# A new order of work around each exchange, with a quarter of it issued by ScalarE, in a fused attention and linear kernel

## What is computed

```python
xn = layernorm(x)
q = (xn @ wq.T)                        # 16 heads, 128 "nope" + 64 rotary columns
kv_lat, k_pe = split(xn @ wkv_a.T)     # 128 + 64
q_lat = einsum('bshd,hdc->bshc', q_nope, wkv_b_h[:, :128])
kv_cache = rmsnorm(kv_lat, kv_norm_w)
scores = (q_lat . kv_cache + rope(q_pe) . rope(k_pe)) * SCALE, causal
attn = softmax(scores)
out_lat = einsum('bsht,btc->bshc', attn, kv_cache)
out = einsum('bshc,hdc->bshd', out_lat, wkv_b_h[:, 128:]) @ wo.T
result = x + out + (xn @ ternary(weight).T + bias)
```

## Time and profile before

| | |
|---|---|
| runs of the kernel | 2119.6, 2119.89, 2128.14 us; median 2119.89 |
| the profiled execution | 2115.17 us, span 2113.1 us |
| PE busy | 1803.1 us (85%) |
| PEld, DVE, ACT, POOL busy | 1523.3, 1208.9, 853.5, 1004.4 us |
| mean granted clock of TensorE | 0.92 |
| DMA queue of SP | 48.6% of 16 DMA engines' span |
| DMA queue of ACT | 5.5% |

### The profile page before, as it was taken

The page is one execution under the profiler, slowest core; times in us unless marked ns, Lnnn a source line. Parts: engine busy times, 40 slices in busy tenths (PEclk is TensorE's granted clock), DMA queues, the critical chain, the costliest instruction groups (busy, mean ns, idle before and its releaser), DMA issues.

```text
span 2113.1 us, 28101 instructions
## 1 busy us (share of the span) xinstructions
PE 1803.1 (85%) x9326; PEld 1523.3 (72%) x9326; DVE 1208.9 (57%) x2801; ACT 853.5 (40%) x1358; POOL 1004.4 (48%) x635
## 2 busy tenths in 40 slices
PE   6997888778989979889888898788898888888885
PEld 5786666657777767777777777677677777777775
DVE  5764566646666655656465555455555555555552
ACT  4552443433444433344444434243443434334342
POOL 4763444434554554454444545344444544445443
PEclk9888899989999999999999999898999989999998
DMA  6992555547656565654444535546455455453544
GB/s 226 356 315 100 147 141 157 162 133 186 169 151 161 148 190 138 168 134 116 119 125 121 136 102 132 158 98 174 112 121 125 104 128 123 114 131 95 127 105 102
DMA packets 127183, 309.11 MB, mean 146 GB/s; under 512 B 29442, under 2 KB 41987, under 8 KB 125508
## 3 DMA queue, kind: packets, MB, share of 16 engines
q1 hardware_dynamic: 117152, 273.20, 48.6%
q10 hardware_dynamic: 9892, 34.18, 5.5%
HBM read 113.28 MB, written 34.60 MB: 70 GB/s over the span
## 4 chain that ended last, share of the span: by engine, by line
PE 28%; issue 20%; POOL 13%; SPq 12%; ACT 8%; DMA 5%; DVE 5%; POOLq 0%; ACTq 0%; DVEq 0%
SPq L986 11%; PE p_score L1101 10%; PE p_out L1121 9%; POOL pT L1367 7%; DMA pT<-turned 5%; PE p_result L1133 4%; DVE turned L1192 3%; ACT pT_h L1286 3%; PE p_lat L1081 3%; ACT probs L1275 3%; POOL qp_l L1356 3%; POOL qp_l L1359 3%; PE p_rot L1081 2%; ACT qp_h L1310 2%; DVE probs L1170 1%
## 5 line engine op out<-in xcount | busy, mean ns | idle before, releaser
L1367 POOL TENSOR_TENSOR pT<-pT,pT_h 128x1024 fp32r<-128x1024 f32 x320 | 684.1, 2164 | 576.4 <-ACT pT_h L1286 574.3
L1170 DVE TENSOR_SCALAR_CACHE_REDUCE probs<-p_score 128x512 f32<-128x512 f32 (+3 forms) x640 | 382.8, 602 | 617.7 <-PE p_score L1101 435.3
L1121 PE MATMUL p_out<-pT_h,V_h 128*128 128x256 f32 (+3 forms) x1024 | 327.9, 320 | 198.0 <-DVE o_l L1219 103.4
L1286 ACT ACTIVATE pT_h<-pT 128x1024 fp32r<-128x1024 f32 x320 | 291.4, 963 | 451.7 <-DMA pT<-turned 296.1
L1275 ACT ACTIVATE probs<-probs,neg_max 128x128 f32<-128x128 f32 (+15 forms) x256 | 307.0, 1199 | 378.9 <-DVE neg_max L1176 376.8
L1121 PEld LDWEIGHTS p_out<-pT_h,V_h 128*128 128x128 f32 x1024 | 213.2, 208 | 235.3 <-DVE o_l L1219 116.1
L1192 DVE STREAM_TRANSPOSE turned<-probs 128x1024 f32<-128x1024 f32 (+7 forms) x384 | 341.5, 915 | 28.2 <-ACT probs L1275 23.4
L1121 PE MATMUL p_out<-pT,V_h 128*128 128x256 f32 (+3 forms) x1024 | 323.0, 315 | 0.0
L1121 PE MATMUL p_out<-pT_h,V_l 128*128 128x256 f32 (+3 forms) x1024 | 321.8, 314 | 0.0
L1101 PE MATMUL p_score<-Kn_h,q_h 128*128 128x512 f32 (+3 forms) x640 | 249.4, 390 | 18.0 <-DVE q_l L1215 18.0
L1101 PE MATMUL p_score<-Kp,qp_h 128*128 128x512 f32 (+3 forms) x640 | 242.6, 379 | 21.3 <-POOL qp_l L1359 20.5
(11 more groups left out here) (135 smaller groups left out, 2390.0 us busy)
## 6 DMA issues: line engine op xcount, KB each, us to landing
pT<-turned SPq DMA_DIRECT2D x512, 128.0 KB, 2.3
Wq<-wq_scr ACTq DMA_DIRECT2D x63, 512.0 KB, 4.5
Wv<-wv_scr SPq DMA_DIRECT2D x63, 512.0 KB, 3.6
pT<-turned SPq DMA_DIRECT2D x256, 112.0 KB, 2.3
pT<-turned SPq DMA_DIRECT2D x256, 96.0 KB, 2.2
pT<-turned SPq DMA_DIRECT2D x256, 80.0 KB, 2.1
pT<-turned SPq DMA_DIRECT2D x256, 64.0 KB, 2.5
Wp<-wp_scr SPq DMA_DIRECT2D x31, 512.0 KB, 4.3
```

The source lines that it names most:

```text
L1121: mm = pe.matmul(out[:, :, cols, :], v[:, t, :], pt[:, :, t - first, rest, :], start=(t == 0 and a == 0), stop=(t == piece_tiles(s) - 1 an ...
L1170: dve.tensor_scalar(probs[row % ROW_RING][:, b * CW:b * CW + width], p_score[n % SCORE_RING][:, 0:width], SCALE, LOWEST, ALU.mult, ALU.max ...
L1286: act.activation(high.rearrange("p r t i q -> p r t (i q)"), low.bitcast(F32).rearrange("p r t i q -> p r t (i q)"), ACT.Copy).then_inc(p_ ...
L1367: pool.tensor_tensor(low.rearrange("p r t i q -> p r t (i q)"), low.bitcast(F32).rearrange("p r t i q -> p r t (i q)"), high.bitcast(F32). ...
```

## The change

- In the matmul queue the value groups of a piece move from units 2, 3, 4 to 3, 4, 5 in stage 3 and from units 1, 3, 5, 7 to 3, 4, 5, 6 in stage 4; stages 1 and 2 stay. The output projections of stage 4 move from units 2, 3, 4, 5 to 0, 1, 2, 2. `p_lat` moves one unit ahead in stage 4, `p_rot` ahead of the first scores in stage 1 and to unit 1 in stage 4.
- `high_group` and `low_group` move from unit 0 of slot s+2 to its unit 1 in stages 1 and 3, and from the last unit of slot s+1 to unit 0 of slot s+2 in stage 4. `split_output` and `high_output` follow the last value group: unit 0 of slot s+3 instead of unit 5 of s+2 in stage 3, unit 7 of s+2 instead of unit 0 of s+3 in stage 4.
- DVE turns the last row of a piece at unit 0 of the next slot in all stages; before at unit 1 from slot 17 on.
- ACT makes each exponential ahead of the query and rotary splits of the same unit, and that of a slot's last row at the slot's end.
- SP issues three quarters of each exchange, 12 DMAs. ACT issues the fourth with four DMAs (`exchange_last`), behind the same two waits, at unit 1 of the next slot (unit 0 up to slot 16).
- In stage 1 all five rotary operations stand in unit 0 on DVE, the sum in unit 1 and the splits in unit 2.

```diff
 def value_unit(s, k):
-    return (2 + k, 1 + k, 2 + k, 1 + 2 * k)[phase(s)]
+    return (2 + k, 1 + k, 6 - groups_of(s - 2) + k, 3 + k)[phase(s)]
...
     if k < HIGH_RING:
-        return (s + 2, 0) if phase(s + 1) in (0, 2) else (s + 1, units_of(s + 1) - 1)
+        return (s + 1, units_of(s + 1) - 1) if phase(s + 1) == 1 else (s + 2, 0 if phase(s + 1) == 3 else 1)
...
-    return 2 + i if s % 2 == 0 else i
+    return 0 if s % 2 else (2 + i if phase(s) == 2 else (0, 1, 2, 2)[i])
...
                 if 1 <= s <= SLOTS:
-                    exchange(s - 1, (2, 3))
+                    exchange(s - 1, (2,))
...
                 for u in range(units_of(s)):
+                    rotary = u == rotary_unit(s) and opens_head(s) and g % 2 and g + 1 < HEADS
+                    if rotary and s < H:
+                        project_rotary(g + 1)
                     if s < SLOTS:
                         scores(g, unit_of_head(s, u))
-                    if u == 0 and opens_head(s) and g % 2 and g + 1 < HEADS:
+                    if rotary and s >= H:
                         project_rotary(g + 1)
...
-                    if 1 <= s <= SLOTS and u == (1 if s > H else 0):
+                    if 1 <= s <= SLOTS and u == 0:
                         turn_row(head_of(s - 1), first_row(s - 1) + rows_of(s - 1) - 1)
...
+            def exchange_last(s):
+
+                g, tiles = head_of(s), piece_tiles(s)
+                act.wait_ge(blocked, QB * g + first_row(s) + rows_of(s))
+                need(act, pv_done, groups_before(s - 1) if s >= 1 else 0)
+                for r in range(4):
+                    act.dma_start(slots(pT[s % 2][96:P, :], s)[:, r, 0:tiles, :, :].bitcast(F32),
+                                  slots(turned[s % 2][32 * r:32 * (r + 1), :], s)[:, 3, 0:tiles, :, :]
+                                  ).then_inc(exchanged[s % 2], 16)
...
                 for u in range(units_of(s)):
-                    if u == query_unit(s) and g + 1 < HEADS:
-                        high_query(g + 1)
-                        if g + 2 < HEADS:
-                            load_q(g + 2)
                     for old in (s - 3, s - 2):
                         if 0 <= old < SLOTS and (s, u) == split_place(old):
                             high_output(old)
...
                             if (s, u) == high_place(old, k):
                                 high_group(old, k)
+                    if s < SLOTS and (u + 1) % (chunk_of(g) + 1) == 0 and u + 1 < units_of(s):
+                        exp_row(g, first_row(s) + u // (chunk_of(g) + 1))
+                    if u == query_unit(s) and g + 1 < HEADS:
+                        high_query(g + 1)
+                        if g + 2 < HEADS:
+                            load_q(g + 2)
                     if u == rotary_high_unit(s) and g + 1 < HEADS:
                         high_rotary(g + 1)
-                    if s < SLOTS and (u + 1) % (chunk_of(g) + 1) == 0:
-                        exp_row(g, first_row(s) + u // (chunk_of(g) + 1))
+                    if 1 <= s <= SLOTS and u == (1 if s > H else 0):
+                        exchange_last(s - 1)
+                if s < SLOTS:
+                    exp_row(g, first_row(s) + rows_of(s) - 1)
```

More of the change, by code:

```diff
@@ L179, in latent_unit, with rotary_unit @@
         return (1 + it // 2, 2 + it)[phase(s)]
-    return (it if phase(s) == 2 else 1 + it) if s < SLOTS and closes_head(s) else None
+    return it if s < SLOTS and closes_head(s) else None
 def query_unit(s):
     if s < 2 * H:
-        return (3, 6)[phase(s)]
-    return (4 if phase(s) == 2 else 5) if s < SLOTS and closes_head(s) else None
+        return (2, 6)[phase(s)]
+    return 4 if s < SLOTS and closes_head(s) else None
 def rotate_ops(s, u):
     if phase(s) == 0:
-        return ((), (0, 1, 2), (3, 4), ())[u]
-    return ((0,), (1, 2), (3, 4))[u - 1] if 1 <= u <= 3 else ()
+        return range(5) if u == 0 else ()
+    first = rotary_unit(s) + 1
+    return ((0,), (1, 2), (3, 4))[u - first] if first <= u <= first + 2 else ()
+def rotary_unit(s):
+    return 1 if phase(s) == 3 else 0
 def rotary_add_unit(s):
-    return (2 if phase(s) == 0 else 4) if opens_head(s) else None
+    return (1, 4, 4, 5)[phase(s)] if opens_head(s) else None
 def rotary_high_unit(s):
-    return (3 if phase(s) == 0 else 5) if opens_head(s) else None
+    return (2, 5, 5, 6)[phase(s)] if opens_head(s) else None
 def row_unit(s, i):
```

## The result

| | before | now | forecast |
|---|---|---|---|
| median of the runs | 2119.97 us (2119.6 to 2128.14) | 1893.19 us (1886.6 to 1894.48) | 1925 |
| ratio, 95% interval | | 0.8916 (0.8886 to 0.8946) | 0.908 |
| profiled execution, span | 2115.17, 2113.1 | 1894.48, 1892.0 | 1920 |
| PE busy | 1803.1 us (85%) | 1717.4 us (91%) | |
| mean granted clock | 0.92 | 0.97 | |

The account below looks back on a forecast made before the run. Stage 4 was held to be set by a closed loop through the exchange, not PE's work; terms -96-74-30+8-3 = -195 took the profiled 2115.17 to 1920, plus 4.7 for the median: 1925 us, 8-in-10 range 1880 to 2025.

Parts of the forecast that it names:

- The loop in stage 4: Fourth query chunk: exchange, pT_h, exp, o_h, o_l, turn, next exchange; one round of 22.3 us sets the slot.
- A: Rival, exchanges: transfers, not issues, set them, so data still lands late; 1963 us, chance 0.2.
- B: Rival, stages 3 and 4: ACT-POOL chain 1.2 us later than walked, PE waits in all 64 slots; 2022 us, chance 0.18.
- C: Rival, ACT's queue: wait for data delays exchange_last behind it, a self-feeding loop; about 2235 us, chance 0.05.
- D: Rival, stages 1, 3, 4: acc and o_l in time, no new waits; 1848 us, half of it 1887, chance 0.07.
- Stage 4: Fourth query chunk: 600 us against 695.9, from 569 of full-clock slots, 19 waiting for acc, 12 for lower clock.
- Stage 3: Third query chunk: 484 us against 557.9, from 449 of full-clock slots, 15 for o_l, 10 clock, 10 boundary.
- Stage 2: Second query chunk: 336 us against 366.5; order unchanged but for turn and exchange, pT waits mostly go.
- Stage 1: First query chunk: +8 us; per pair of slots +2.5 for acc, +0.5 for clock, -1.8 for q_l, 7 pairs.
- The quarter on ACT: Exchange issues: with all 16 on SP data lands 2.5 us later, costing 22 us in stage 3, 16 in stage 4.
- the cover: Stage 4: the exchange lands at least 1.7 us before the next slot's first pT_h wants it.
- the tail: End of the kernel, behind the stages: 3 us less for the shorter last exchange.

Follow-up runs that it names:

- Run 5: Changed kernel with the exp of a slot's last row put back behind the next slot's three pT_h, stage 4 only: 1974.61 us, ratio 0.9303.
- Run 7: Changed kernel with ACT's query and rotary splits ahead of the exp of their unit again, stage 2 only: 1882.68 us, ratio 0.8864.
- the control: The changed kernel timed again, unaltered, on the chip of the experiments: 1894.49 us, ratio 0.8936 to the kernel before.
- run 1: Changed kernel's new order with all 16 DMAs of an exchange issued on SP, none on ACT: 1906.45 us, ratio 0.897 to the kernel before.
- run 2: Kernel before, in its old order, with only a quarter of each exchange moved to ACT: 2040.87 us, ratio 0.9615.
- run 3: Kernel before with only the exp of a slot's last row moved ahead of the three pT_h, stage 4 only: 2103.58 us, ratio 0.9908.
- run 4: Changed kernel with half of each exchange, eight DMAs, issued on ACT instead of a quarter: 1944.3 us, ratio 0.9153 to the kernel before.

## Why the prediction was right, and where its terms were off

- *The loop in stage 4: right.* It said that one round of exchange, pT_h, exp, o_l and turn sets the slot and that the moves cut it. Run 5 puts one link back and loses 79 us; the windows show PE as the bound. Rivals A and B would leave a wait of ACT for data or of PE for POOL's pT in most slots; stage 4 has neither, but for one of 1.68 us at its end. C needed issues over 1.5 us; ACT's have a median of 0.635. D, with no new waits, had 1887 for half of its terms: the waits for acc and o_l did come, smaller, and their share for a lower clock did not. One reading of the prediction is wrong: the slot at clock 0.87 has one standstill, of 5.76 us, and not two. That the total is only 32 us off is in part luck: stages 1, 3 and 4 were forecast 46 us too long and stage 2 21 us too short.
- *Stage 4: 22 us too long.* PE's full-clock slots are 18.98, 17.70, 16.84 and 17.70, that is 71.2, where 71.1 was said. The wait for acc is there, but 0.94 and 0.30 us in a slot instead of 2.4, so 10 to 12 us in place of 19: 7 less. The 12 us for a lower clock behind it did not come: the slot with the wait has clock 1.00. The last 3 are slots at the stage's ends.
- *Stage 3: 14 us too long.* The wait for o_l is 1.2 us and not 1.85 (6 less), it drew no lower clock (10 less), the slots with no wait are 15.00 and 13.90 instead of 15.29 and 14.06 (6 less), and the stage's ends cost 18 and not 10 (8 more). Its row, from 870 to 1230:

```profile
PE p_result L1138 <- DVE o_l L1227: 8.2, 7, 1.2
```

- *Stage 2: 21 us too short, the worst term.* That the order is unchanged but for the turn and the exchange was wrong. The wait for pT in even slots did go, as said; but ACT's exp had moved ahead of q_h inside a unit, and PE waits for acc there in both slots, 0.86 and 0.73 us (13 us in the 8 pairs). Before, PE had one such wait in the stage, of 0.51 us. Run 7 takes this away; the kernel is 10.5 us faster for it. The rest: one slot (the fourth) where ACT waits 8.4 us for its data while the chunk's store and load run, some 5 us, and busy slots 0.4 us a pair longer, 3 us. Of this part the control has less (its stage is 353 us), so it is an estimate.
- *Stage 1: 10 us too long.* The wait of 3 us for acc was predicted at 3.2 and measured at 3.03:

```profile
363.90 0.73 PE L1138 MATMUL p_result<-Wv,o_h 128*128 128x512 f32 x2 [3.03 <-DVE acc L1241]
```

  What was left out is what it replaces. Per pair of slots the kernel before had four waits of PE, 0.88 twice for q_l, 1.62 for qp_l and 0.67 for acc; the prediction counted only the first two as going. Now there are 3.03 and 1.06: 4.1 against 4.05, and nothing is left of the 8 us. The charge for the clock was right in kind: beside four of the stage's seven standstills of 3.03 us, and beside all seven in the control, stands a stretch at 1.2 GHz.
- *The quarter on ACT: some 10 us, not 38.* The stages differ here. In stage 4 the exchange got shorter by 1.1 us (median from first issue to last landing 13.1 in run 1, 12.0 now) and not by 2.5; both queues issue more slowly side by side. And the cover was larger than walked: the slot is 17.7 us or more and not 16.4, since it has its own wait or its longer neighbour; in run 1 ACT waits for no data from 1340 to 1820. In stage 3 the exchange did get shorter by 2.2 us (12.5 and 10.3), and in run 1 ACT is late in 17 of 32 slots; but POOL's low parts still come before PE wants them, so the step that failed is the one from ACT's lateness to PE's. (The 16 us for stage 4 are also mis-added: 0.8 x 0.7 x 32 is 18.) The Trainium skill ("DMA: Bandwidth & Descriptors", Issuing engines are not separate DMA queues) lets a second issuing engine save only the sequencer's time; by it the prediction said that the 2.5 us shrink to almost nothing in stage 4. The trace agrees with the rule: what is saved is 2.2 us in stage 3 and 1.1 in stage 4, never more than the 2.5 of issuing, and stage 4 is 4 us shorter for it. What the saved time is worth depends on the order around it: in run 2, where a loop holds the exchange, about 1 us less in every slot is worth 82 us.
- *The rest:* the tail is 5.5 us shorter, where 3 was said. The stages and the tail make 27 of the 32 us; of the others most is that the median, taken 4.7 us above the profiled execution, is 1.3 below it now.

## What to carry to other kernels

When an engine's queue waits for data at a fixed place, ask which instructions behind that place make the next data: if the next transfer depends on them, the slot is as long as the round trip, whatever the busiest engine needs, and moving one link ahead of the wait may only bring up the next one (run 3). Shortening a transfer pays most as long as it lies in such a loop; afterwards it was worth little (run 1), and further issues cost the queue that they stand in (run 4). And when reordering within a unit of work, follow each pair of neighbours in the queue to who waits for the second of them; in stage 2 that was worth about as much as the quarter of the exchange.

## What the runs showed of the hardware that was not expected

**Two issuing engines slow each other in stage 4, but not in stage 3.** The exchange's issues in the changed kernel, line 991 on SP and line 1293 on ACT (ns min/median/max), each with the us to landing:

```profile
L991 SPq DMA_DIRECT2D pT<-turned x1152: 507/592/1915, 205.9 to 1867.1; - x192
...
DMA to landing us min/median/max: 1.9/3.2/9.6
...
L1293 ACTq DMA_DIRECT2D pT<-turned x384: 514/635/1627, 205.9 to 1861.0; - x192
```

The median issue is as long as before (0.59 and 0.64 us), and the median landing is 3.2 instead of 2.3 us; with all on SP again it was 2.4. In stage 4, where a DMA moves 112 or 128 KB, SP's 12 issues fill a median of 9.0 us: while ACT issues too, three of SP's stand 0.94 to 1.05 us apart instead of 0.64. In stage 3, with 80 or 96 KB, nothing of this is seen; 12 and 4 issues of one exchange there:

```profile
983.90 7.50 SPq L991 DMA_DIRECT2D pT<-turned  x12
...
983.91 2.71 ACTq L1293 DMA_DIRECT2D pT<-turned  x4
```

The whole exchange, from first issue to last landing, has medians of 12.5 us in stage 3 and 13.1 in stage 4 with all on SP (run 1), 10.3 and 12.0 with a quarter on ACT, 8.1 and 10.9 with half on ACT (run 4). So in stage 4 a second issuing engine gives back less than half of the issue time that it takes over. Whether the size of the DMAs makes the difference wasn't tried.

**Standstills of 1.2 us left the clock alone, those of 3 us did not always.** In stages 3 and 4 of the kernel before the records of the clock show 45 stretches at 1.2 GHz, 201 us in sum, each beside a standstill of PE; the shortest of these is 1.8 us, the longest 5.8, and 7.8 at a chunk's boundary. Now there are 2 stretches, 14 us, beside standstills of 2.5 and 9.3 us. The seven standstills of 1.2 us in stage 3 and those under 1 us in stage 4 have none. Between the two lies no clear line: in stage 4 one of 2.91 us had none. In stage 1 a standstill of 3.03 us comes every second slot. The first window, over two slots with one of them, still has the full clock; the same two slots in the control, with the same standstill, haven't:

```profile
347.00:378.00 31.00, 26.42 (x135) 21.09 (x135) 20.32 (x52) 13.19 (x29) 13.65 (x9) 1.00 0.58 155
...
348.00:379.00 31.00, 26.64 (x130) 21.32 (x129) 19.95 (x51) 12.74 (x28) 13.65 (x9) 0.94 0.52 149
```

PE's busy time has fallen by 86 us (1803.1 to 1717.4) with as many matmuls to do, while the time at 1.2 GHz fell from 338 to 119 us over the whole span. The 86 us are 39% of the 221 us that the span lost: as an estimate, for no run varied the clock alone, that much of the gain came by way of the clock.
